# Opening of a two-layer graph network on one Trainium2 core: message rows first, in half chunks, and the self term's products behind them

## The reference

```python
h = relu(layernorm(x))
# layer 0
m_data, m_ctrl = h[src] @ W_data.T + b_data, h[src] @ W_control.T + b_control
msg = where(edge_type == 0, m_data, m_ctrl)
x = x + relu(segment_sum(msg, dst) + (h @ W_self.T + b_self))
# layer 1
h = relu(layernorm(x))
g = tanh(h[dst] @ gate_w[:128] + h[src] @ gate_w[128:] + gate_b)
yn = tanh(w * yes_weight + (1 - w) * no_weight)
x = x + segment_sum(h[src] * ((g + yn) * 0.5 * d[dst] * d[src])[:, None], dst)
```

## Time and profile before

| | |
|---|---|
| median of three runs | 5841.05 us |
| profiled execution, its time | 5829.9 us |
| its span (first to last instruction) | 5828.1 us |
| granted TensorE clock, mean | 0.872 |
| busy shares: PE, DVE, ACT, POOL | 74%, 75%, 52%, 74% |
| POOL's first fetch of layer 0 | 124.41 us |

### The profile page before, as it was taken

One profiled execution on the slowest core, in us unless ns is written; L12 is line 12 of the kernel. 1 busy time (PEld: TensorE's weight loads), 2 busy tenths in 40 slices (PEclk: granted clock), 3 DMA queues, 4 the chain that ended last, 5 costly groups with the idle time before them and its releaser, 6 DMA issues.

```text
span 5828.1 us, 119944 instructions
## 1 busy us (share of the span) xinstructions
PE 4286.3 (74%) x29542; PEld 3197.4 (55%) x29542; DVE 4365.5 (75%) x16525; ACT 3038.4 (52%) x10494; POOL 4307.3 (74%) x4285
## 2 busy tenths in 40 slices
PE   6588888888888888875577777777777777777754
PEld 5355666655565555553455555555555555555543
DVE  7887777878787777755467777777777777777863
ACT  5666666666666666643254544544445444444530
POOL 5777777777777777777457777777777777777774
PEclk8599999999999999987688888888888888888875
DMA  7777777777777777776355455555555455455544
GB/s 239 245 217 223 222 224 223 225 221 223 225 225 224 223 223 222 220 224 203 102 134 121 118 118 119 121 119 120 119 119 121 119 119 119 118 120 118 120 97 116
DMA packets 764988, 979.91 MB, mean 168 GB/s; under 512 B 135667, under 2 KB 567063, under 8 KB 763799
## 3 DMA queue, kind: packets, MB, share of 16 engines
q1 hardware_dynamic: 620131, 687.26, 40.0%
q0 software_dynamic: 135168, 281.42, 19.7%
q10 hardware_dynamic: 9012, 3.56, 0.2%
HBM read 911.05 MB, written 60.67 MB: 167 GB/s over the span
## 4 chain that ended last, share of the span: by engine, by line
POOL 72%; issue 23%; PE 2%; DVE 2%; DMA 1%; SPq 1%; ACTq 0%; DVEq 0%; POOLq 0%; ACT 0%
POOL G L570 72%; SPq L311 1%; PE PS L883 0%; DMA OWF<-in_x 0%; DMA out<-OWF 0%; DVE ST L1172 0%; DVE OHF L1183 0%; DVE G L1639 0%; PE PS L891 0%; DMA G<-t,IDXB 0%; PE PS L1054 0%; PE PS L1057 0%; DVE OWF L1191 0%; DVE OWF L1832 0%; PE PS L1081 0%
## 5 line engine op out<-in xcount | busy, mean ns | idle before, releaser
L570 POOL DMA_INDIRECT G<-t,IDX x4016 | 4019.1, 1001 | 1274.3 <-issue 1223.0
L1081 PE MATMUL PS<-CDST,HTB 128*128 128x256 f32 x2352 | 868.3, 455 | 447.7 <-DVE CDST L1768 419.9
L705 ACT ACTIVATE OHF<-PS 128x384 bf16<-128x384 f32 x1764 | 864.6, 490 | 515.7 <-PE PS L927 488.0
L939 PE MATMUL PS<-CDST,OHF 128*128 128x256 bf16 x5292 | 901.0, 281 | 35.0 <-DVE ACC L1283 35.0
L797 ACT ACTIVATE ST<-PS,MV 128x1 f32<-128x1 f32 x1764 | 457.5, 259 | 720.2 <-issue 327.6
L1072 PE MATMUL PS<-HTB,OWF 128*128 128x129 f32 x3528 | 815.1, 317 | 9.7 <-DVE OWF L1747 9.7
L1072 PEld LDWEIGHTS PS<-HTB,OWF 128*128 128x128 f32 x3528 | 720.5, 218 | 166.8 <-issue 75.9
L1081 PEld LDWEIGHTS PS<-CDST,HTB 128*128 128x128 f32 x2352 | 408.0, 217 | 556.0 <-ACT HTB L816 510.4
L939 PEld LDWEIGHTS PS<-CDST,OHF 128*128 128x128 bf16 x5292 | 532.6, 101 | 315.8 <-issue 68.7
L1081 PE MATMUL PS<-OHF,OWF 128*128 128x256 f32 x1176 | 438.6, 459 | 246.5 <-DVE OHF L1768 230.2
L1300 DVE TENSOR_SCALAR CDST<-IO,BASE 128x256 bf16<-128x256 int16 x1764 | 510.8, 305 | 5.0 <-PE PS L939 4.1
(11 more groups left out here) (240 smaller groups left out, 8316.9 us busy)
## 6 DMA issues: line engine op xcount, KB each, us to landing
HTB<-t0s SPq DMA_DIRECT2D x442, 384.0 KB
OWF<-t0s SPq DMA_DIRECT2D x440, 384.0 KB
HTB<-t SPq DMA_DIRECT2D x882, 132.0 KB
G<-t,IDX POOLq DMA_INDIRECT x4016
YN<-rows SPq DMA_DIRECT2D x882, 64.0 KB
OHF<-rows SPq DMA_DIRECT2D x882, 64.0 KB
t0s<-HTB SPq DMA_DIRECT2D x25, 384.0 KB
t0s<-OWF SPq DMA_DIRECT2D x24, 384.0 KB
```

What stands on the lines that cost most here:

```text
L570: eng.indirect_dma_start(out=G[:, k:k + width], out_offset=None, in_=table, in_offset=bass.IndirectOffsetOnAxis(ap=at, axis=0)).then_inc(s ...
L705: eng.activation(X0[:, k % KX, :, :].rearrange("p n w -> p (n w)"), PS[:, cell_bank(k), 0:384], ACT.Identity).then_inc(q_ev, 1)
L939: ins = eng.matmul(PS[:, 4, 0:DW], X0[:, k % KX, n, :], CD0[:, k % KD, :], start=b == 0 and n == 0, stop=b == NB - 1 and n == 2)
L1081: eng.matmul(PS[:, 4 + g % 2, 0:DW], X1[k % KX1], CD1[k // 2 % 3][:, k % 2, :], start=b == 0, stop=b == NB - 1).then_inc(d_ap, 1)
```

## The change

- **Half chunks.** A chunk's 7 blocks are worked on as 4 and 3 (`HALF`) by PE's transposes and message products, by ACT's relu, by DVE's rows and by SP's stores to `t0`. The PSUM regions keep their size, and each half has its own semaphore count (o_t, o_h, o_m, o_y), so one half can be filled while the other is emptied.
- **Order.** PE does no self products until the message products of all 14 chunks are issued. The relu's results therefore stay: they go to the lower half of `ACC` (`HT0`) and no longer to two buffers. The self products then read 448 columns at a time from there, and ACT writes the start values over them. On SP the 14 stores to `ini` stand behind all stores to `t0` and behind the wait for their landing. DVE's wait for `ini` moves from the front of the edge loop to its first additions.
- **DVE.** `rows` follows three chunks behind instead of four; `windows` stands behind all rows. `scales` first copies the mean into PSUM (`MP`), and the operation behind it reads it from there.
- **SP.** `dst` is loaded behind x's fifth chunk instead of its third, `src` now in front of it; `typ` is loaded in front of the third chunk's store instead of the fifth; the store of zeros stands in front of the 13th chunk's.
- The other lines only follow the new counts of semaphores.

```diff
+HALF = ((0, 4), (4, CB))
...
+        HT0 = blocks(ACC[:, 0, 0:NB * 128])
+        MP = PS[:, 2, 0:NB]
...
+        def stored(c):
+
+            return 32 * (c // 2 + 1) + 16 * (c == NC - 1)
...
-                if c == 2:
-                    load(STI, dst, s_dst)
                 if c == 3:
                     load(IDX[:, :], src, s_src)
+                if c == 4:
+                    load(STI, dst, s_dst)
+
+            def table_half(c, first, last):
+                eng.wait_ge(o_y, 2 * c + 1 + (first > 0))
+                whole = min(last, NB - 1 - c * CB)
+                at = (c * CB + first) * 128
+                eng.dma_start(t0[at:at + (whole - first) * 128, :].rearrange("(b p) w -> p b w", p=128),
+                              YB[c % 2][:, first:whole, :]).then_inc(a_t0[c % 2], 16)
+                if whole < last:
+                    eng.dma_start(t0[(NB - 1) * 128:N, :], YB[c % 2][0:NL, whole, :]).then_inc(a_t0[c % 2], 16)
+
             for c in range(NC):
-                if c == 4:
+                if c == 2:

                     eng.wait_ge(s_stg, 1)
                     load(STI, typ, s_typ)
-                eng.wait_ge(a_ye, c + 1)
-                chunk_dma(eng, YB[c % 2], t0, c, False, a_t0[c % 2])
-                if c >= 1:
-                    eng.wait_ge(a_se, c)
-                    eng.dma_start(ini[:, (c - 1) * CB * 128:c * CB * 128],
-                                  ACC[:, 0, (c - 1) * CB * 128:c * CB * 128]).then_inc(s_ini, 16)
-            eng.wait_ge(a_se, NC)
-            eng.dma_start(ini[:, (NC - 1) * CB * 128:], ACC[:, 0, (NC - 1) * CB * 128:NB * 128]).then_inc(s_ini, 16)
-            eng.wait_ge(s_zr, 1)
-            eng.dma_start(t0[N:NB * 128, :], ZR[0:NB * 128 - N, :]).then_inc(s_zr, 16)
+                if c == NC - 2:
+                    eng.wait_ge(s_zr, 1)
+                    eng.dma_start(t0[N:NB * 128, :], ZR[0:NB * 128 - N, :]).then_inc(s_zr, 16)
+                for first, last in HALF:
+                    table_half(c, first, last)
             eng.wait_ge(s_zr, 17)
             for c in (NC - 2, NC - 1):
-                eng.wait_ge(a_t0[c % 2], landed(c, 2))
-            eng.wait_ge(a_h, NC)
-            eng.wait_ge(a_m, NC)
+                eng.wait_ge(a_t0[c % 2], stored(c))
+            for c in range(NC):
+                eng.wait_ge(a_se, c + 1)
+                eng.dma_start(ini[:, c * CB * 128:(c + 1) * CB * 128],
+                              ACC[:, 0, c * CB * 128:(c + 1) * CB * 128]).then_inc(s_ini, 16)
+            eng.wait_ge(o_h, 2 * NC)
+            eng.wait_ge(o_m, 2 * NC)
...
-                eng.wait_ge(a_t, c + 1)
+                eng.wait_ge(o_t, 2 * (c + 1))
...
-                eng.wait_ge(a_t0[c % 2], landed(c, 2))
+                eng.wait_ge(a_t0[c % 2], stored(c))
...
+            def positive(c):
+                for n, (first, last) in enumerate(HALF):
+                    eng.wait_ge(o_t, 2 * c + n + 1)
+                    eng.activation(HT0[:, c * CB + first:c * CB + last, :], strip(0)[:, first:last, :], ACT.Relu)\
+                       .then_inc(o_h, 1)
...
             normal(0)
-            eng.wait_ge(s_w, 16 * 9)
-            for c in range(NC + 1):
+            root(2, 0)
+            positive(0)
+            normal(1)
+            for c in range(1, NC):
                 if c + 2 < NC:
                     root(c + 2, 0)
                 if c + 1 < NC:
                     normal(c + 1)
-                if c < NC:
-                    eng.wait_ge(a_t, c + 1)
-                    if c >= 2:
-                        eng.wait_ge(a_m, c - 1)
-                    eng.activation(HTB[:, c % 2, :, :], strip(0), ACT.Relu).then_inc(a_h, 1)
-                if c >= 1:
-                    eng.wait_ge(a_ms, c)
-                    eng.activation(blocks(ACC[:, 0, (c - 1) * CB * 128:c * CB * 128]),
-                                   strip(2), ACT.Identity, bias=BS[:, 0:1]).then_inc(a_se, 1)
+                positive(c)
+            eng.wait_ge(s_w, 16 * 9)
+            for c in range(NC):
+                eng.wait_ge(a_ms, c + 1)
+                eng.activation(ACC[:, 0, c * CB * 128:(c + 1) * CB * 128].rearrange("p (a w) -> p a w", a=2),
+                               PS[:, c % 2 * 2:c % 2 * 2 + 2, 0:CB * 64], ACT.Identity, bias=BS[:, 0:1]).then_inc(a_se, 1)
             for c in (NC - 2, NC - 1):
...
-            def turn(c):
+            def turn(h):
+                c, (first, last) = h // 2, HALF[h % 2]
                 eng.wait_ge(a_n, c + 1)
-                if c >= 1:
-                    eng.wait_ge(a_h, c)
-                for i in range(CB):
+                if h >= 2:
+                    eng.wait_ge(o_h, h - 1)
+                for i in range(first, last):
                     ins = eng.transpose(strip(0)[:, i, :], XR[:, c * CB + i, :], IDENT[:, :])
-                ins.then_inc(a_t, 1)
+                ins.then_inc(o_t, 1)
+
+            def messages(h):
+                c, (first, last) = h // 2, HALF[h % 2]
+                eng.wait_ge(o_h, h + 1)
+                if h >= 2:
+                    eng.wait_ge(o_y, h - 1)
+                for i in range(first, last):
+                    ins = eng.matmul(strip(4, 256)[:, i, :], HT0[:, c * CB + i, :], W2[:, :], start=True, stop=True)
+                ins.then_inc(o_m, 1)

             turn(0)
+            turn(1)
+            for h in range(2 * NC):
+                messages(h)
+                if h + 2 < 2 * NC:
+                    turn(h + 2)
             for c in range(NC):
-                if c + 1 < NC:
-                    turn(c + 1)
-                eng.wait_ge(a_h, c + 1)
-                if c >= 1:
-                    eng.wait_ge(a_se, c)
-                for i in range(CB):
-                    ins = eng.matmul(strip(2)[:, i, :], WS[:, :], HTB[:, c % 2, i, :], start=True, stop=True)
+                if c >= 2:
+                    eng.wait_ge(a_se, c - 1)
+                for n in range(2):
+                    at = c * CB * 128 + n * CB * 64
+                    ins = eng.matmul(PS[:, c % 2 * 2 + n, 0:CB * 64], WS[:, :], ACC[:, 0, at:at + CB * 64],
+                                     start=True, stop=True)
                 ins.then_inc(a_ms, 1)
-                if c >= 1:
...
-                    eng.wait_ge(a_ye, c)
-                for i in range(CB):
-                    ins = eng.matmul(strip(4, 256)[:, i, :], HTB[:, c % 2, i, :], W2[:, :],
-                                     start=True, stop=True)
-                ins.then_inc(a_m, 1)
...
-            eng.wait_ge(a_ye, NC)
+            eng.wait_ge(o_y, 2 * NC)
...
             def rows(c):
-                eng.wait_ge(a_m, c + 1)
-                if c >= 2:
-                    eng.wait_ge(a_t0[c % 2], landed(c - 2, 2))
-                eng.tensor_tensor(YB[c % 2], strip(4, 256),
-                                  BB[:, :].unsqueeze(1).broadcast_to([128, CB, 256]), ALU.add)\
-                   .then_inc(a_ye, 1)
+                for n, (first, last) in enumerate(HALF):
+                    eng.wait_ge(o_m, 2 * c + n + 1)
+                    if c >= 2 and n == 0:
+                        eng.wait_ge(a_t0[c % 2], stored(c - 2))
+                    eng.tensor_tensor(YB[c % 2][:, first:last, :], strip(4, 256)[:, first:last, :],
+                                      BB[:, :].unsqueeze(1).broadcast_to([128, last - first, 256]), ALU.add)\
+                       .then_inc(o_y, 1)

             def scales(c):
                 cols = slice(c * CB, (c + 1) * CB)
                 eng.wait_ge(a_sq, c + 1)
+                eng.tensor_copy(MP[:, cols].unsqueeze(2), MV[:, cols, 0:1])
                 link(eng.reciprocal(RS[:, cols], SQ[:, cols]))
-                eng.scalar_tensor_tensor(DG[:, cols].unsqueeze(2), MV[:, cols, 0:1], -1.0, RS[:, cols].unsqueeze(2),
+                eng.scalar_tensor_tensor(DG[:, cols], MP[:, cols], -1.0, RS[:, cols],
                                          ALU.mult, ALU.mult).then_inc(a_rs, 1)
...
-            for c in range(NC + 4):
+            for c in range(NC + 3):
                 if c < NC:
                     stats(c, XR[:, c * CB:(c + 1) * CB, :], a_x[c], landed(c))
                 if 1 <= c <= NC:
                     scales(c - 1)
-                if c == 4:
+                if c == 3:
                     eng.wait_ge(s_w, 16 * 9)
-                if c >= 4:
-                    rows(c - 4)
-                if c == NC + 1:
-                    windows()
-
+                if c >= 3:
+                    rows(c - 3)
+            windows()
             eng.tensor_tensor(YD[:, :], YW[:, :], NW[:, :], ALU.subtract).then_inc(s_bg, 1)
             eng.wait_ge(s_q, 11)
             cell_targets()
             for c in (NC - 2, NC - 1):
-                eng.wait_ge(a_t0[c % 2], landed(c, 2))
+                eng.wait_ge(a_t0[c % 2], stored(c))
             eng.wait_ge(s_z, NC + 2)
-            eng.wait_ge(a_se, NC)
-            eng.wait_ge(a_m, NC)
```

(11 more changed lines are left out.)

5 lines of the change are left out of this document (2 added, 3 removed).

## The result

| | before | changed |
|---|---|---|
| median of six runs | 5842.56 us | 5818.02 us |
| lowest and highest | 5837.81, 5857.13 | 5809.58, 5826.5 |
| profiled execution, span | 5828.1 us | 5820.9 us |
| first fetch of layer 0 in it | 124.41 us | 102.45 us |

The ratio of changed to before is 0.9956, with a 95% interval from 0.9942 to 0.9970: 24.5 us faster by the medians, and clear of noise. The forecast was 5819 us with the first fetch at 101.8.

The account below looks back on a forecast made before the run. POOL's fetches set the loops' pace, so an earlier first fetch counts in full: entry 22.6 us sooner, at 101.8, less 1 us for slowed fetches. 5841.05 - 21.6 = 5819 us, 8 in 10 range 5806 to 5838.

Parts of the forecast that it names:

- The opening counts in full: Loops go at POOL's pace, so bringing the first fetch forward, by 22.6 us, brings the end forward as much.
- What held DVE's last rows: Before the change, DVE's last rows waited 4.89 us for PE, which does 1.73 us of self products a chunk.
- The start at 41.1: DVE stands still before chunk 2's rows until the first store to t0 lands, about 41.1 us; earlier gains are lost.
- DVE's work a chunk: Statistics and reciprocal 2.17, L1199 0.2, copy 0.2, rows in two pieces 2.1: 4.67 us a chunk, DVE setting the pace.
- The allowance of 0.5 us a chunk: Added to DVE's pace because each half waits for one of another engine; between 0 and 0.76 us.
- The tail: After chunk 13's scales: normalization 2.8, half a relu 0.5, PE 6.9, last half of rows 0.9; 11.1 us, until 96.8.
- The issue and landing behind it: From DVE's last rows to POOL's entry: 4.5 us from issue to entry plus 0.5 for one more issue, entry 101.8.
- The copy: Copying the mean to PSUM takes 0.2 us; the rival (0.12) has it wait for POOL as L1199 did, time 5829.
- POOL's own work: With dst landing at about 25, index work ends at 78 and clears near 92, under 101.8: no cost.
- Fetches beside DVE: windows and cell_targets run beside the first seven fetches and slow them: 1 us taken, up to 5 possible.
- The late loop: Other engines start some 21 us late, covered by POOL's five slots (28.2 us), no cost; rival (0.10): 5826 to 5834.
- The slower case: Rival (0.06): PE falls to 1.2 GHz in the standstill before 41.1 and stays there, bounding the chunks: 5856 us.

Follow-up runs that it names:

- experiment 1: The changed kernel without the copy of the mean to PSUM, the operation reading both inputs from SBUF again: first fetch at 111.69 us, 9.2 later than changed.
- experiment 2: The kernel before with the operation that waits for POOL (minus mean times reciprocal) replaced by a second reciprocal: first fetch at 118.91 us, 5.5 sooner than before.
- experiment 3: The changed kernel with self products back between the messages and two reciprocals for copy and operation: first fetch at 106.96 us, 4.5 later than changed.
- experiment 4: The changed kernel with whole chunks instead of halves and PE's old order of transposes: first fetch at 122.99 us.
- experiment 6: The changed kernel with DVE's rows four chunks behind instead of three: first fetch at 93.73 us, one run.
- experiment 7: The changed kernel with rows four chunks behind and windows in front of chunk 2's rows: first fetch at 93.80 us, ratio to before 0.9958.
- experiment 10: The changed kernel with rows four chunks behind and windows in the standstill, timed on another chip: first fetch at 94.71 us, ratio to before 0.9944.
- experiment 12: The kernel before with only SP's order of the zeros and ini stores changed: first fetch at 123.57 us, 0.8 sooner.

## Why the prediction was right, point by point

- **The opening counts in full.** Right: 21.96 us at the first fetch, 24.5 in the medians. Experiments 1 to 4 were run once each, but their first fetches and the 401st kept the same distances within 2.1 us where POOL sets the pace: 639.67, 633.4, 630.59 and 646.99 for experiments 2, 1, 3 and 4, against 645.0 before and 624.36 changed.
- **What held DVE's last rows.** The reading was incomplete. I took the 4.89 us in front of them for PE's self products. But PE itself stood 4.19 us for DVE's rows of chunk 12, and these stood behind `windows` (experiment 2). The sum doesn't use that reading, since it is built from the new order, in which `windows` is behind.
- **The start at 41.1.** Right: 40.97.
- **DVE's work a chunk.** Summed 4.67, in fact 4.33 (experiment 6). From start to start, statistics, copy and reciprocal take 2.24 us instead of 2.37, L1230 0.08 instead of 0.2, and the rows 2.01 instead of 2.1.
- **The allowance of 0.5 us a chunk.** The pace came out at 5.21 against my 5.17, so the scales of chunk 13 ended at 85.6 against 85.7. But the reason was wrong. I called it small waits of halves for one another; it is one ring through ACT's, PE's and DVE's lists, 10.42 us for two chunks, and it gives 0.88 us over DVE's own 4.33. From 40.97 on DVE waited 6.8 us where I had put 4.5, and worked 37.8 where I had summed 40.1. Two errors cancelled, which is luck. Because I did not see the ring, I expected 103.5 to 107 from whole chunks and they gave 122.99, and a lag of four was not in my mind.
- **The tail.** 11.1 summed, 12.8 measured (85.6 to 98.4). The path was another: not the scales of chunk 13 but those of chunk 12 (83.0) lead to the end, over ACT, and from 86.56 PE works without a break through the messages of three chunks until 97.4. The issue and landing behind it: 5.0 summed, 4.0 measured (98.4 to 102.45). So 1.7 us too little and 1.0 too much.
- **The copy.** 0.155 us and never a wait; that rival is out. Experiment 1 gives what it saves, 9.2 us.
- **POOL's own work.** `dst` at 24.88 against 25, index work done at 75.2 against 78. No cost, as said.
- **Fetches beside DVE.** Mis-sized: I took 1 us between 0 and 5. L1186 held one fetch by 0.5 us and L1195 one by 3.1: 3.6 us. Of the lead, 3.3 us were gone at the eighth fetch, 2.2 at the 41st and 1.3 at the 401st. The Trainium skill's inference ("SBUF — State Buffer", "Who interferes with whom") that a two-input operation doesn't hold descriptor generation is not what these rows show: the fetch issued at 109.41, inside L1195 (109.11 to 112.63), ended at 113.45, 0.82 us behind it, and in experiments 7, 10 and 12 the fetch beside that operation took 4.10, 4.11 and 2.95 us. The measurement decides.
- **The late loop.** SP's first loads at 119.98 against 121, first sums at 120.52. No fetch of the first 400 waited for PE by more than 0.3 us, as said. The cover of 28.2 us was misread: the fetch at 299.29 is the 133rd, in step 16 counted from 0, and step 12's slot was used again by the 137th at 304.28, 33.2 us behind. The least of the first 20 steps was 32.2 us before (step 15: 303.12 to 335.28) and 20.5 in the changed kernel (295.65 to 316.17). So the late loop uses up some 12 us of the cover, and in this execution 20 us are left. Both numbers are counts over the traces.
- **PE's clock** fell in the standstill and came back: after PE had stood 9.82 us, the messages of half a chunk took 3.75 us at 42.34, at a granted clock of 0.50 (1.2 GHz), and 1.97 at 48.78, at 1.00. The slower case did not come, and the self products ran at 1.00.

What each part is worth with all others in place: the copy 9.2 us, the self products' place 4.5, the halves (at a lag of three, and with the transposes' place) 20.5, all against 22 in sum. They don't add up, because each part only moves the bound to the next ring. The place of `windows`, about 5 us by estimate, was not tested alone, nor was the place of `dst`.

## What to carry to other kernels

When three engines pass chunks around with in-order lists, write down the ring: which instruction stands in front of which in each list, over how many chunks it closes, and divide. The busy times say only what the pace can't be under; the lag of one stage in one list decided here between 4.3, 5.2 and 6.5 us a chunk. And an instruction of 0.17 us that takes 1.38 on the mean is worth a look at where its operands lie before anything is reordered.

## What the runs showed of the hardware

A VectorE operation with two SBUF inputs and a GpSimd computation that reads SBUF hold each other up both ways. VectorE waits until the running GpSimd operation ends (3.21, 4.09, 3.29 us for 7 numbers), and with one input in PSUM it doesn't (166 ns on the mean). Beside GpSimd's clears, which only write, it doesn't wait either: 0.17 us at 86.73 in the kernel before and at 81.92 in experiment 1. A long VectorE operation of that kind also holds an indirect DMA's issue for the rest of its time (4.04 instead of 0.95 us) and a GpSimd computation too: in experiment 7, POOL's L557 began at 33.76 beside L1175 (32.86 to 36.87) and took 5.54 instead of 2.54 us. The fetches' mean of about 1.00 us against 0.94 undisturbed may hold more of it, over 4016 fetches; that was not tried.
